# Two interleaved attention chains replaced by one chain on three rotating PSUM pairs

## The reference

```python
scores = jnp.einsum('bhqd,bhkd->bhqk', Qh, Kh) / jnp.sqrt(jnp.float32(dk))
scores = jnp.where(causal, scores, jnp.float32(-1e+30))
attn = jax.nn.softmax(scores, axis=-1)
out = jnp.einsum('bhqk,bhkd->bhqd', attn, Vh)
return jnp.concatenate(head_outs, axis=-1) @ W_O
...
x = _layernorm(x + _L0_attn_ref(x, ...), axis=-1)
```

## Time and profile before

| | us |
|---|---|
| median of the 3 runs | 6487.3 |
| lowest, highest | 6213.19, 6673.82 |
| the profiled execution | 6213.19 |
| its span, core 5 (the slowest) | 6211.7 |
| spans of the eight cores | 6172.4 to 6211.7 |
| mean granted TensorE clock of the cores | 0.890 to 0.896 |

### The profile page before, as it was taken

How to read it: one execution, slowest core, us unless ns; L and a number is a source line. 1 busy time by engine, 2 the same in 40 slices (tenths; PEclk the granted TensorE clock), 3 DMA queues, 4 the chain that set the end, 5 groups by cost and what they waited for, 6 DMA issues and landing times.

```text
span 6211.7 us, 61961 instructions; the slowest of 8 cores (6172.4 to 6211.7 us)
## 1 busy us (share of the span) xinstructions
PE 4789.6 (77%) x20400; PEld 1837.3 (30%) x20400; DVE 1848.0 (30%) x2803; ACT 1176.2 (19%) x1301; POOL 440.5 (7%) x811
## 2 busy tenths in 40 slices
PE   0879797465655777776499999788849999978884
PEld 0333333011111111112144444333314444433331
DVE  0212212234333222222444445300044544430004
ACT  0000000465504777772000000000000000000000
POOL 0000000000000000000000000122200000002220
PEclk9999998677676888888699999999969999999996
DMA  9232325300241000005145544599934554458993
GB/s 151 47 56 50 59 46 119 95 26 30 46 130 46 31 31 31 31 23 136 27 89 97 100 96 95 107 191 187 188 92 89 99 98 95 89 105 189 183 189 101
DMA packets 357663, 573.56 MB, mean 92 GB/s; under 512 B 85808, under 2 KB 208880, under 8 KB 354288
## 3 DMA queue, kind: packets, MB, share of 16 engines
q0 software_dynamic: 157488, 260.75, 27.2%
q1 hardware_dynamic: 199872, 308.85, 16.0%
HBM read 741.90 MB, written 88.28 MB: 134 GB/s over the span
## 4 chain that ended last, share of the span: by engine, by line
PE 51%; DMA 18%; DVE 12%; ACT 11%; issue 6%; another core or an unknown queue 2%; DVEq 0%; ACTq 0%; SPq 0%; POOLq 0%; POOL 0%
PE ps L734 14%; PE ps L744 14%; ACT ar L551 9%; DMA ar<-wd 8%; PE ps L861 7%; DMA vspill<-ar 7%; PE ps L343 4%; PE ps L586 3%; DVE ar L564 3%; PE ps L528 2%; DMA ar<-wospill 2%; PE ps L436 2%; PE ps L660 1%; PE ps L1038 1%
## 5 line engine op out<-in xcount | busy, mean ns | idle before, releaser
L734 PE MATMUL ps<-ar 128*128 128x512 bf16 x4096 | 1221.2, 380 | 59.0 <-DMA ar<-wg 31.1
L744 PE MATMUL ps<-ar 128*128 128x512 bf16 x4096 | 1220.6, 380 | 1.0 <-DMA ar<-wu 1.0
L861 PE MATMUL ps<-ar 128*128 128x512 bf16 x4096 | 938.0, 385 | 188.5 <-DMA ar<-wd 114.8
L551 ACT ACTIVATE ar<-ps 128x1024 bf16<-128x1024 f32 x960 | 918.7, 1051 | 307.7 <-PE ps L536 290.3
L586 PE MATMUL ps<-ar 128*65 128x512 bf16 x1920 | 654.1, 425 | 206.2 <-DVE ar L564 197.6
L861 PEld LDWEIGHTS ps<-ar 128*128 128x128 bf16 x4096 | 391.1, 99 | 735.5 <-issue 320.5
L564 DVE TENSOR_TENSOR ar<-ar 128x512 bf16<-128x512 bf16 x768 | 324.0, 425 | 922.4 <-ACT ar L551 879.1
L734 PEld LDWEIGHTS ps<-ar 128*128 128x128 bf16 x4096 | 401.2, 98 | 545.2 <-issue 63.7
L744 PEld LDWEIGHTS ps<-ar 128*128 128x128 bf16 x4096 | 401.3, 98 | 486.7 <-issue 5.0
L528 PE MATMUL ps<-ar 64*128 64x512 bf16 x960 | 401.1, 423 | 144.7 <-DMA ar<-qspill 113.7
L764 ACT ACTIVATE ar<-ps 128x1024 bf16<-128x1024 f32 x128 | 131.0, 1023 | 1609.1 <-PE ps L734 965.7
(11 more groups left out here) (103 smaller groups left out, 2704.6 us busy)
## 6 DMA issues: line engine op xcount, KB each, us to landing
ar<-hspill SPq DMA_DIRECT2D x512, 256.0 KB, 4.8
ar<-wg POOLq DMA_DIRECT2D x128, 512.0 KB, 6.5
ar<-wu POOLq DMA_DIRECT2D x128, 512.0 KB, 8.8
ar<-wd POOLq DMA_DIRECT2D x512, 128.0 KB, 5.0
ar<-wospill SPq DMA_DIRECT2D x72, 512.0 KB, 3.4
hspill<-ar SPq DMA_DIRECT2D x128, 256.0 KB, 6.6
ar<-xT POOLq DMA_DIRECT2D x8, 2048.0 KB, 19.4
ar<-xTo POOLq DMA_DIRECT2D x8, 2048.0 KB, 16.2
```

The source lines that it names most:

```text
L551: lambda e, b0=b0, eap=eap: e.activation(eap, ps[:, b0 * 512:(b0 + 2) * 512], AF.Exp, scale=0.125),
L734: lambda e, bb=bb, th=th, kc=kc, s=s, wgs=wgs: e.matmul(bank(bb + th), wgs[:, kc * 128:(kc + 1) * 128], x1[:, kc * 2048 + s * 512: kc * 20 ...
L744: lambda e, bb=bb, th=th, kc=kc, s=s, wus=wus: e.matmul(bank(bb + 2 + th), wus[:, kc * 128:(kc + 1) * 128], x1[:, kc * 2048 + s * 512: kc ...
L861: lambda e, bi=bi, ft=ft, th=th, ic=ic, wst=wst, hst=hst: e.matmul(bank(bi), wst[:, ft * 128:(ft + 1) * 128], hst[:, th * 512:(th + 1) * 512],
```

## The change

The pairs of slots and the chains go. One loop runs over the four slots, in it one over the 12 head pairs, and all of a slot's steps for a head pair form one chain. The score banks are three pairs (0 to 5) taken in turn by steps and finalizations together (`prot`), the output banks are 6 and 7. AV stands three steps behind its score instead of one. K and V are loaded anew for each slot, EXT[s] blocks of them, still double-buffered by head pair; Q of all 12 head pairs comes in one load per slot; the residual has a buffer of its own and is loaded at the slot's start. The finalization has the same operations in the same order, written in the loop, on the rotating pair. The projection runs behind each slot, in two groups of eight output tiles with 6 and 12 loads of W_O, 18 a slot; then comes the slot's norm. The instructions of a step, of a finalization and of a norm are unchanged. The diff, cut to its core:

```diff
+    xos = A(xos_o, NCK * 512)
+    qb = A(qb_o, HPN * 512)
+    ob = A(ob_o, HPN * 512)
...
-    for sp_ in range(2):
-        sA, sB = 2 * sp_, 2 * sp_ + 1
-        chains = []
-        for ci, (s, pair, obank, oboff, mB, moff) in enumerate(
-                ((sA, (0, 1), (6, 7), ob_o, "msk", msk_o),
-                 (sB, (2, 3), (4, 5), ob2_o, "msk2", ring_o))):
-            c = Chain()
-            c.s, c.pair, c.obank, c.oboff = s, pair, obank, oboff
-            c.ext = EXT[s]
-            c.mB, c.moff = mB, moff
-            c.avq = []
-            chains.append(c)
-        for c in chains:
-            mw = B[c.mB].wr_waits()
...
-            qsl = hp % 4
-            qrB = B["qr"][qsl]
-            qstg = A(qb_o + qsl * 1024, 1024)
-            qw = qrB.wr_waits()
-            dma("sync", "ql%d" % qsl, qstg[:, 0:512], qspill[sA, hp], waits=qw)
-            dma("sync", "ql%d" % qsl, qstg[:, 512:1024], qspill[sB, hp], waits=())
-            qrB.note_write(("ql%d" % qsl, kb.cnt["ql%d" % qsl]))
...
+    for s in range(4):
+        ext = EXT[s]
+        ev = dma("gpsimd", "xos",
+                 xos.rearrange("p (c t) -> p c t", c=NCK),
+                 cm(xTo)[:, :, s * 512:(s + 1) * 512],
+                 waits=B["xos"].wr_waits())
+        B["xos"].note_write(ev)
+
+        evql = dma("sync", "ql",
+                   qb.rearrange("p (h q) -> p h q", h=HPN),
+                   qspill[s].rearrange("h p q -> p h q"),
+                   waits=B["qb"].wr_waits() + B["qspill"].rd_waits())
+        B["qb"].note_write(evql)
+
+        mw = B["msk"].wr_waits()
+        dma("sync", "mk", A(msk_o, 2048), msk[2 * s + 0], waits=mw)
...
+            kstg = A(kst_o + kpar * 4096, ext * 512)
+            vstg = A(vst_o + kpar * 4160, 130 * 4 * ext)
...
-                c.avq.append(do_av)
-                if len(c.avq) > 1:
-                    c.avq.pop(0)()
...
-                    if j < cA.ext:
-                        chain_step(cA, j, sub, cA.pair)
-                    solo = j >= cA.ext
-                    if solo and j == cA.ext and sub == 0:
-                        while cA.avq:
-                            cA.avq.pop(0)()
-                    pair = cB.pair if (not solo or (j * 4 + sub) % 2 == 0) \
-                        else cA.pair
-                    chain_step(cB, j, sub, pair)
-            for c in chains:
-                while c.avq:
-                    c.avq.pop(0)()
-                _finalize_hp(kb, B, A, bank, kb_cnt=None, c=c, hp=hp,
-                             e_o=e_o, sm32=sm32, rowb=rowb, onesr=onesr, AFv=AF,
-                             ALUv=ALU)
-
...
+                    pr = prot[0] % 3
+                    prot[0] += 1
+                    b0 = 2 * pr
+                    w = (kB.rd_waits() + B["qb"].rd_waits()
+                         + B["bank"][b0].wr_waits() + B["bank"][b0 + 1].wr_waits())
+                    kb.emit("tensor",
...
+                    avq.append(do_av)
+                    if len(avq) > 3:
+                        flush_av()
+            while avq:
+                flush_av()
+            fo = 86144
+            fB = B["efin"]
+            fw = B["bank"][6].rd_waits() + B["bank"][7].rd_waits()
...
+            pr = prot[0] % 3
+            prot[0] += 1
+            bb0 = 2 * pr
...
-        xosbufs = (A(xosr_o, NCK * 512), A(vst_o, NCK * 512))
-        xBs = (B["xos"], B["xos2"])
-        for ci, c in enumerate(chains):
-            xB = xBs[ci]
-            kvw = (B["kst"][0].wr_waits() + B["kst"][1].wr_waits()) if ci == 0 \
-                else (B["vst"][0].wr_waits() + B["vst"][1].wr_waits())
-            evxo = dma("gpsimd", "xos" if ci == 0 else "xos2",
-                       xosbufs[ci].rearrange("p (cc t) -> p cc t", cc=NCK),
-                       cm(xTo)[:, :, c.s * 512:(c.s + 1) * 512],
-                       waits=xB.wr_waits() + kvw)
-            xB.note_write(evxo)
-        for grp4 in range(4):
-            fms = list(range(4 * grp4, 4 * grp4 + 4))
-            nho_g = max((2 if fm < 2 else (6 if fm < 8 else HPN)) for fm in fms)
...
+        for grp in range(2):
+            fms = list(range(8 * grp, 8 * grp + 8))
+            nho = 6 if grp == 0 else HPN
...
+                            bank(i), wst[:, fm * 128:(fm + 1) * 128],
+                            ob[:, ho * 512:(ho + 1) * 512],
...
-            for ci2 in range(2):
-                for i, fm in enumerate(fms):
-                    bi = 4 * ci2 + i
-                    xB = xBs[ci2]
...
-        for kBx in B["kst"] + B["vst"]:
-            for sname, v in (B["xos"].wr_waits() + B["xos2"].wr_waits()):
-                kBx.note_read((sname, v))
...
-def _finalize_hp(kb, B, A, bank, kb_cnt, c, hp, e_o, sm32, rowb, onesr,
-                 AFv, ALUv):
-    fo = 86144
-    fB = B["efin"]
-    b6, b7 = c.obank
-    p0, p1 = c.pair
```

More of the change, by code:

```diff
@@ new lines, in build_program @@
+            fB.add_write(ev6)
+            B["bank"][6].note_read(ev6)
+            B["bank"][7].note_read(ev6)
+            ev1 = kb.emit("scalar",
+                          lambda e, fo=fo: e.activation(sm32[0:1, 0:512],
+                                                 A(fo, 512, r0=64, rows=1), AF.Ln),
+                          waits=fB.rd_waits() + B["sm"].wr_waits(), inc="sa")
+            ev2 = kb.emit("scalar",
+                          lambda e, fo=fo: e.activation(sm32[0:1, 512:1024],
+                                                 A(fo + 512, 512, r0=64, rows=1), AF.Ln),
+                          waits=(), inc="sa")
@@ new lines, in build_program @@
+            B["row"].note_write(ev4)
+            B["sm"].note_read(ev4)
+            pr = prot[0] % 3
+            prot[0] += 1
+            bb0 = 2 * pr
+            evb = kb.emit("tensor",
+                          lambda e, bb0=bb0: e.matmul(bank(bb0), onesr[0:1, :], rowb[0:1, 0:512],
+                                             start=True, stop=True),
+                          waits=B["row"].rd_waits() + B["onesr"].rd_waits()
+                                + B["bank"][bb0].wr_waits() + B["bank"][bb0 + 1].wr_waits(),
+                          inc="sp")
@@ new lines, in build_program @@
+            evb2 = kb.emit("tensor",
+                           lambda e, bb0=bb0: e.matmul(bank(bb0 + 1), onesr[0:1, :], rowb[0:1, 512:1024],
+                                              start=True, stop=True),
+                           waits=(), inc="sp")
+            B["bank"][bb0].note_write(evb)
+            B["bank"][bb0 + 1].note_write(evb2)
+            B["row"].note_read(evb2)
+            B["onesr"].note_read(evb2)
+            evn = kb.emit("vector",
+                          lambda e, hp=hp, fo=fo, bb0=bb0: e.tensor_tensor(
+                              ob[0:64, hp * 512:(hp + 1) * 512],
+                              A(fo, 512, rows=64), bank(bb0, rows=64), ALU.mult),
+                          waits=fB.rd_waits() + [("sp", evb2[1])]
+                                + B["ob"].wr_waits(),
+                          inc="sv")
@@ new lines, in build_program @@
+            evn2 = kb.emit("vector",
+                           lambda e, hp=hp, fo=fo, bb0=bb0: e.tensor_tensor(
+                               ob[64:128, hp * 512:(hp + 1) * 512],
+                               A(fo + 512, 512, rows=64), bank(bb0 + 1, rows=64), ALU.mult),
+                           waits=(), inc="sv")
+            B["ob"].add_write(evn2)
+            fB.note_read(evn2)
+            B["bank"][bb0].note_read(evn2)
+            B["bank"][bb0 + 1].note_read(evn2)
+        for grp in range(2):
+            fms = list(range(8 * grp, 8 * grp + 8))
+            nho = 6 if grp == 0 else HPN
+            for ho in range(nho):
```

359 lines of the change are left out of this document (139 added, 220 removed).

## The result

| | before | changed |
|---|---|---|
| median, us | 6483.59 (13 executions) | 6328.20 (12 executions) |
| lowest, highest, us | 6213.19, 6673.82 | 6059.34, 6534.52 |
| profiled execution, us | 6213.19 | 6059.34 |
| attention stage, mean of the 8 cores, us | 1931.3 | 1755.7 |
| rest of the span, mean of the 8 cores, us | 4265 | 4275 |

The ratio is 0.9725, with the interval 0.9654 to 0.9796: the changed kernel is faster, by 2.0 to 3.5%. In many executions, of either kernel, the cores of one die, or of both, show a mean granted clock of 0.80 to 0.88 in place of 0.90 and the time is some per cent longer; the ratio is taken over the executions without that, the medians over all of them, and this alone makes 6328 so much more than 6059.

What follows compares the result with a forecast made beforehand. ACT was taken as nearest its limit, with idle time around it. Terms 883 + 371.5 + 67 + 450.8 + 3 + 5 = 1780 us against 1930.6, 150 less: 6213 - 150 = 6063 us; range 5985 to 6205 us.

Steps and rivals of the forecast that it cites:

- The stage's gain: Attention stage, first exp to end of last layer norm: 1780 us against 1930.6, 150 us less.
- The time: Whole kernel: 6063 us, 2.4% less, set against the profiled execution of 6213 us; range 5985 to 6205 us.
- All 960 steps at 0.92 us: Attention steps, masked ones included: neither mask nor AV holds ACT up, 0.92 us each, 883 us.
- Gap 7.64 us: Between a run's last exp and the next run's first: 7.64 us, with 0.10 for a lone exp 48 x 7.74 = 371.5 us.
- Half clock, 67 us: Restarts after gaps: 1.2 us a run in slots 1 to 3, 2.0 in slot 0, together 67 us.
- Attention by slot: Attention of the four slots would take near 203, 282, 371 and 459 us.
- Projection and norm, 453.8 us: Behind each slot: 112.7 us, four times 450.8, plus 3 us for last adds exposed once per slot.
- The start, 5 us: First run of the stage waits for 12 heads of Q and shares DMA with the residual load: 5 us.
- No wait for K, V or Q at the slots' borders: At the three slot borders the next slot's K, V and Q land under the norm; nothing added.
- The clock did not stay low: Rival: PE keeps 1.2 GHz through the runs, every step costs 1.54 us, 6590 us; chance 0.07.
- The restart did not cost 2 to 3 us more a run: Rival: restarts after gaps cost more than the cushion holds, 48 x 2.5 = +120 us, 6180 us; chance 0.20.
- Fetches did not show: Rival: K and V come late at each run, 48 x 5 = +245 us, 6308 us; chance 0.03.

Runs made afterwards that it cites:

- the last section: The changed kernel beside its version with deferred finalization and held-back AVs, on one chip: ratios 0.9748 and 0.9403 to the kernel before.

## Why the prediction was right or wrong, point by point

- **The stage's gain: right.** 150 us were predicted, 169.7 measured on the page's cores (1930.6 - 1760.9), 175.6 as the mean. The ratio of the numbers on record, 6063 / 6213 = 0.976, lies inside the measured interval, 0.9654 to 0.9796.
- **The time: wrong, and the step is the base.** The median is 6328.2 us, above the range 5985 to 6205. The failing step is "the sum stands against the profiled run, the fastest of the three": all terms and the whole range were laid around 6213, though the same sentence names a median of 6487 and an execution of 6674. No term of the kernel's work makes up the 265 us: the 0.976 of the sum, put on the median of before, gives 0.976 x 6483.6 = 6328 us. That this meets the measured 6328 to the microsecond is luck: the medians themselves move, and on the chip of the last section they were 6047 and 6208 us. The range had to hold how executions of one kernel differ, 7% in the three that were shown; mine was 3.6% wide and held only what was unknown about the change.
- **All 960 steps at 0.92 us: right.** 7.37 us for eight masked steps, 24.86 for 27 exps. The prediction argued it from three pairs of banks; they aren't needed for it: with the lag of three, two pairs do it as well.
- **Gap 7.64 us: right.** 7.59 us in 37 of the 44 gaps inside the slots on the page's core, 7.38 to 7.94 in the others, 7.62 on average.
- **Half clock, 67 us: right in sum, a little off by slot.** 2.0 us a run of slot 0 was met (1.98). 1.2 for the others was on average 1.04 (1.36, 0.96, 0.81). 12 x 5.11 = 61 us. On the eight cores the clock falls behind each of the 176 borders inside slots 2 and 3 and is back after 7 to 10 us.
- **Attention by slot.** 203, 282, 371, 459 us predicted; 205.0, 284.8, 369.6, 455 measured.
- **Projection and norm, 453.8 us: right.** 115.3, 109.7, 112.6 and 108.9, together 446.5 us, in which the wait at the slots' borders (below) is counted.
- **The start, 5 us: wrong.** The stage begins no later than before: at 1138.5 us against 1139.4 on the page's cores, 1116.8 against 1116.4 as the mean. Nor could a late first exp have made the stage longer, which is counted from it. K and V of a head pair in slot 0 land about 3 us behind their issue, and Q of the 12 head pairs in 8.1, as the DMA issues of the changed kernel show:

```profile
ar<-kspill SPq DMA_DIRECT2D x12, 256.0 KB, 3.0
...
ar<-qspill SPq DMA_DIRECT2D x4, 1536.0 KB, 8.1
```

- **No wait for K, V or Q at the slots' borders: right.** PE waits for none of them behind the start. What shows there is the norm's tail, from which the second score pair has to get its banks (2 and 3) back: one exp, then 25 us of waiting at each of the three borders, 75 us in all. Neither kernel avoids it (before, ACT waited 37.87 us there); whether the next slot's attention could run under the norm with other banks for it was not tried:

```profile
1434.08 1.02 ACT L547 ACTIVATE ar<-ps 128x1024 bf16<-128x1024 f32 x1 [4.25 <-PE ps L532]
...
1459.00 0.58 PE L524 MATMUL ps<-ar 64*128 64x512 bf16 x1 [25.05 <-DVE ar L1080]
```

- **The rivals.** The clock did not stay low: attention of the slots has 0.70, 0.79, 0.84 and 0.90, rising with the length of the runs. The restart did not cost 2 to 3 us more a run; with two pairs it costs 0.5 to 2.1 us more than with three, 69 us in place of this rival's 120. Fetches did not show. The rule of the Trainium skill (TensorE: Matmul & The Clock Gate, section "A second HAM failure mode: psum-queue depth-cycling"), by which a kernel that cycled through the banks with small waits between its matmuls had its clock swing, was not met inside the runs: three pairs are cycled through 27 exps in 24.86 us, ACT's pace. With half of the steps slowed so, the time had been worked out as 6360 us; the profiled execution took 6059. Where the clock does fall, PE had waited at the finalization: 4.12 us in the rows above, and in the kernel with the deferred finalization 1.22 and 2.12 us close together.
- **What the sum could not say: where the gain comes from.** It was worked out as new total against old total. Taken apart by the rows of the page's cores, against 0.917 us a step: the solo masked parts, 24 x (13.0 - 7.34) = -136 us; all else that the runs of before lose (A's masked steps, the turn to B alone, the restarts), -132; what the changed kernel's runs lose, +64 (both with the 0.1 us of the first exps); the gaps, with each slot's last, +46; borders, projections and norms, -12, in it the 9 us that ACT waited for K and Q. Together -170, the 169.7 measured. So the lag's part is not the solo steps alone: with slots 2 and 3 the sixteen steps with A masked lost 3.6 us a head pair, 2.3 of it the 0.145 us a step of the earlier trace rows and 1.2 the wait at the turn to B alone. The restarts of those slots gave next to nothing: the 32 plain steps at the start of such a head pair lost 2.1 us for one restart, and the two runs of the changed kernel lose 1.8 for two; with two pairs of banks they lose 5.6. In slots 0 and 1 the old restart runs into A's masked steps and can't be read by itself.
- **Outside the stage.** The rest of the span is 4275 us on average against 4265, and 4296.9 on the page's core. The code there is the same; why it took 10 us more was not tested, and in the experiments it moves between 4242 and 4304.

## What to carry to other kernels

Where a step goes through a second engine before its last matmul, work out the cycle from one matmul to the next that waits for it and divide by the steps that it may span; the lag must be large enough that the result is below the pace of the bounding engine (3.38 us / 2, / 3, / 4 here). More lag than that was not tried; the rule gives it nothing to win. Extra score pairs were then a cushion for restarts, not for the steady state. And give a predicted time the spread of the executions that are shown, beside that of the change: here the sum was good to 20 us and the base was off by 270.

## What the runs showed of the hardware

- Two 64-row score matmuls and two 128-row AV matmuls in turn take 0.87 us a step at 2.4 GHz, 0.32 from score to AV and 0.55 from AV to the next score, and 1.54 us at 1.2 GHz. The 18 filler matmuls of 512 columns, all of one form, take 4.05 us with the 0.37 us of the last one, so they start 0.216 us apart. The two score matmuls overlap, so a step would be three such in a row, 0.65 us; the steps take 0.10 and 0.12 us more at the two changes between the forms (0.32 for 0.216, 0.55 for 0.432), and what takes it is not shown. With ACT at 0.92, PE is near its own limit.
- Matmuls whose result nobody reads made the stage shorter by 74 us: they kept the granted clock at 0.92 instead of 0.81, and about half of the gain lay inside the gap itself, where the matmul that spreads the row sums took 0.37 us in place of 0.58.
- Two short waits of PE, 1.22 and 2.12 us some 4 us apart, stood before a fall of the clock to 1.2 GHz at 153 of 176 borders of the kernel with the deferred finalization. With AVs held back the waits were 0.5 and 2.1 us and it fell at 130 of 176; borders with and without the fall have the same waits, so they alone don't settle it.
